# Mixture-of-experts block on one core: maxima first in the prologue, q in long rows, the scale in the selecting matrix, the best sixteen of both tiles at once

## What is computed

```python
att = jnp.einsum('bhqd,bkd->bhqk', q, k) / sqrt(8)          # causal
x = x + softmax(att) @ v @ w_proj                           # x was layer-normed first
q = rmsnorm(layernorm(x)) @ wq.T                            # 2 x 8 heads of 64
sim = jnp.einsum('pbnhd,hkpd->pbnhk', q, keys)              # 2 x 8 x 32 per token
sx, ix = top_k(sim[0], 16); sy, iy = top_k(sim[1], 16)
scores, pk = top_k(sx[..., :, None] + sy[..., None, :], 16) # best 16 of the pairs
h = gelu(xn @ table_down[indices]) * softmax(scores)
out = einsum('bnhk,bnhkd->bnd', h, table_up[indices])
```

## Time and profile before

| | |
|---|---|
| median of 3 runs | 920.95 us (918.83 to 927.84) |
| profiled execution, its own time | 920.11 us |
| its span | 918.3 us |
| busy: PE, DVE, ACT, POOL | 717.5, 758.6, 708.0, 651.5 us |
| first maxima scores start | 31.36 us |
| first exps of attention scores start | 57.32 us |
| first head added on GpSimd in iteration 0 | 131.64 us |
| one iteration of the loop | 49.6 us |

### The profile page before, as it was taken

One profiled execution on the slowest core, in us unless ns is written; L12 is line 12 of the kernel. 1 busy time (PEld: TensorE's weight loads), 2 busy tenths in 40 slices (PEclk: granted clock), 3 DMA queues, 4 the chain that ended last, 5 costly groups with the idle time before them and its releaser, 6 DMA issues.

```text
span 918.3 us, 20833 instructions
## 1 busy us (share of the span) xinstructions
PE 717.5 (78%) x5982; PEld 470.8 (51%) x6014; DVE 758.6 (83%) x2966; ACT 708.0 (77%) x961; POOL 651.5 (71%) x371
## 2 busy tenths in 40 slices
PE   4574578888897979797988889897979797977463
PEld 3433244556474646464655646474646465554323
DVE  3225379989999989898989999998989898979676
ACT  1334388888988989898989889888889898867381
POOL 2012058798797969696979879797969695968662
PEclk9778788999999999999999999999999999888687
DMA  5411312122130403031212112040303121000000
GB/s 158 56 20 29 43 18 51 25 42 38 24 55 10 70 3 67 10 62 18 56 24 50 30 28 52 11 69 9 64 6 62 17 54 24 23 8 19 0 1 11
DMA packets 58160, 32.53 MB, mean 35 GB/s; under 512 B 5904, under 2 KB 57744, under 8 KB 57936
## 3 DMA queue, kind: packets, MB, share of 16 engines
q1 hardware_dynamic: 58128, 32.14, 19.4%
HBM read 19.93 MB, written 5.24 MB: 27 GB/s over the span
## 4 chain that ended last, share of the span: by engine, by line
PE 26%; issue 25%; DVE 24%; ACT 10%; POOL 10%; DMA 1%; SPq 1%; DVEq 1%; POOLq 0%; ACTq 0%
DVE prob L1010 8%; POOL acc L499 6%; PE score L1308 5%; ACT prob L707 4%; DVE late_scores L865 3%; PE misc L1232 2%; PE misc L1331 2%; PE score L1323 2%; ACT late_scores L595 2%; PE score L1271 2%; PE score L1212 2%; DVE halves L859 2%; DVE ranked L909 1%; PE misc L1259 1%; DVE cand L958 1%
## 5 line engine op out<-in xcount | busy, mean ns | idle before, releaser
L499 POOL TENSOR_TENSOR acc<-acc,prob 128x1024 f32<-128x1024 f32 x186 | 442.5, 2379 | 16.6 <-DVE prob L1010 0.5
L1010 DVE SCALAR_TENSOR_TENSOR prob<-score,cut,prob 128x1024 f32<-128x1024 f32 x256 | 317.9, 1279 | 24.6 <-ACT prob L707 23.3
L707 ACT ACTIVATE prob<-score,neg_lse,unit 128x1024 f32<-128x1024 f32 x256 | 301.5, 1202 | 21.9 <-PE score L1308 19.6
L1308 PE MATMUL score<-sel,pieces_t 128*128 128x512 f16 x512 | 164.4, 407 | 62.5 <-DVE prob L1010 59.1
L499 POOL TENSOR_TENSOR acc<-prob 128x1024 f32<-128x1024 f32 x31 | 73.2, 2361 | 103.5 <-DVE prob L1010 103.5
L612 ACT ACTIVATE probs<-score 128x512 f32<-128x512 f32 x192 | 110.4, 596 | 46.5 <-PE score L1214 42.5
L1308 PEld LDWEIGHTS score<-sel,pieces_t 128*128 128x128 f16 x512 | 40.0, 102 | 128.1 <-DVE prob L1010 115.1
L1271 PE MATMUL score<-xn_kept,wdt 128*128 128x128 f32 x480 | 85.0, 278 | 3.9 <-DVE prob L1010 3.5
L1271 PEld LDWEIGHTS score<-xn_kept,wdt 128*128 128x128 f32 x480 | 72.4, 191 | 29.7 <-issue 6.7
L1214 PE MATMUL score<-cb 128*128 128x256 bf16 (+1 forms) x192 | 60.7, 316 | 26.6 <-DMA q_stack<-max_t 17.0
L1182 PE MATMUL score<-k_ahead,q_ahead 128*128 128x256 bf16 (+1 forms) x512 | 70.7, 251 | 10.5 <-DMA q_ahead<-q_scratch 8.3
(11 more groups left out here) (130 smaller groups left out, 1402.3 us busy)
## 6 DMA issues: line engine op xcount, KB each, us to landing
q_ahead<-q_scratch SPq DMA_DIRECT2D x96, 64.0 KB
q_stack<-q_scratch SPq DMA_DIRECT2D x96, 64.0 KB
q_scratch<-qk_piece SPq DMA_DIRECT2D x16, 192.0 KB, 2.4
xin<-x SPq DMA_DIRECT2D x16, 128.0 KB, 4.2
xres<-x SPq DMA_DIRECT2D x16, 128.0 KB, 4.7
x_kept<-x SPq DMA_DIRECT2D x16, 128.0 KB, 2.0
out<-fin SPq DMA_DIRECT2D x16, 128.0 KB, 5.6
xn_kept<-xn_t SPq DMA_DIRECT2D x15, 128.0 KB, 2.0
```

The costliest lines, as they stand in the source:

```text
L499: eng.tensor_tensor(acc[:, j, :], so_far, prob[:, j * FH + h, :], ALU.add).then_inc(acc_added, 1)
L707: eng.activation(prob[:, g, :], score[g % BUFS][:, :], ACT.Exp, bias=neg_lse[:, j, h:h + 1], scale=unit[:, :]).then_inc(prob_made, 1)
L1010: eng.scalar_tensor_tensor(prob[:, g, :], score[g % BUFS][:, :], cut[:, j, h:h + 1], prob[:, g, :], ALU.is_ge, ALU.mult).then_inc(prob_mas ...
L1308: ins = eng.matmul(score[g % BUFS][:, cols], pieces_t[:, j, h, :], sel[:, cols], start=True, stop=True)
```

## The change

Three things, in the words of the code.

The prologue: the row of maxima (`place_max_row`) is issued before the pieces of the next batch are stored; x of batch 2 is loaded before `stack_pieces(0)`; POOL makes the low piece of batch 0 before the norm of batch 1; the first batch's k copies into `k_ahead` are issued by ACT (`first_keys_ahead`); DVE folds the maxima of batch 0 ahead of the remainder of batch 1; the projection of batch 2 stands ahead of batch 0's key scores; `place_tops(0)` stands ahead of the attention exps of iteration 0; `keep_busy` goes from 40 matmuls to 30.

Long rows: the columns of `w_attn` are reordered on the way in so that heads are inside the width, and `q_scratch` is stored piece by piece. Each row of `q_ahead` and `q_stack` is then one run of 8 KB, and three transfers (of 24, 16 and 8 rows) take the place of six.

The scale and the best sixteen: `unit` is rounded to a power of two and multiplied into a bf16 copy of `sel` (`sel_unit`), so L707 loses its scale operand and `cut` is scaled by one small new instruction (`scale_cut`). `shift_best`, `best_exp`, `sum_best`, `log_sum` and `log_sum_exp` each do both tiles at once; three DVE instructions less and one more (`scale_cut`) per iteration. `ln1` goes ahead of `norm_x2`, and the small instructions move to other places.

```diff
-        q_scratch = nc.dram_tensor("q_scratch", (P, 3, T), BF16, kind="Internal").ap()
+        q_scratch = nc.dram_tensor("q_scratch", (3, P, T), BF16, kind="Internal").ap()
...
-                view = q_scratch.rearrange("(h d) s t -> s d h t", d=HD)
-                for c in range(len(Q_PIECE)):
-                    eng.dma_start(q_ahead[c * HD:(c + 1) * HD, :, :], view[Q_PIECE[c]]).then_inc(ahead_in, 16)
+                rows = q_scratch.rearrange("s (d h) t -> (s d) (h t)", d=HD)
+                for c, count in Q_RANGES:
+                    eng.dma_start(q_ahead[c * HD:(c + count) * HD, :, :].rearrange("r h t -> r (h t)"),
+                                  rows[0:count * HD]).then_inc(ahead_in, 16)
...
                 store_pieces(0)
                 look_ahead(0)
+                load_x(2)
                 stack_pieces(0)
                 load_residual(0)
-                load_x(2)
+                place_max_row(0)
                 store_pieces(1)
                 look_ahead(1)
-                place_max_row(0)
                 stack_pieces(1)
+                place_max_row(1)
                 store_pieces(2)
                 look_ahead(2)
-                place_max_row(1)
...
                 make_xhat(0)
+                qk_low_piece(0)
                 make_xhat(1)
-                qk_low_piece(0)
+                make_xhat(2)
                 qk_low_piece(1)
-                make_xhat(2)
...
+            def first_keys_ahead():
+                eng.wait_ge(stack_cleared, 4)
...
+                for c in range(len(K_PIECE)):
+                    eng.dma_start(k_ahead[c * HD:(c + 1) * HD, :],
+                                  qk_piece[D - 2 * HD:D - HD, K_PIECE[c], T:2 * T]).then_inc(ahead_in, 16)
...
-                eng.activation(prob[:, g, :], score[g % BUFS][:, :], ACT.Exp, bias=neg_lse[:, j, h:h + 1],
-                               scale=unit[:, :]).then_inc(prob_made, 1)
+                eng.activation(prob[:, g, :], score[g % BUFS][:, :], ACT.Exp,
+                               bias=neg_lse[:, j, h:h + 1]).then_inc(prob_made, 1)
...
+            def scale_cut(b):
...
+                eng.tensor_scalar(cut[:, :, :], cut[:, :, :], unit[:, :], None, ALU.mult).then_inc(cut_scaled, 1)
...
-                    ins = eng.matmul(score[g % BUFS][:, cols], pieces_t[:, j, h, :], sel[:, cols],
+                    ins = eng.matmul(score[g % BUFS][:, cols], pieces_t[:, j, h, :], sel_unit[:, cols],
                                      start=True, stop=True)
...
-                keep_busy(score[1], 40)
+                keep_busy(score[1], 30)
...
-                xn_transpose(0, y_t_made, 0)
-                key_scores(0, 0, x2_made, 0)
+                eng.wait_ge(y_t_made, every(y_t_made, 0))
+                project_qkv(2, x2_made, 0)
+                xn_transpose(0, v_next_made, 2)
+                eng.wait_ge(qk_high, every(qk_high, 2))
+                key_scores(0, 0, qk_rest_made, 2)
                 key_scores(0, 1, xn_t_made, 0)
-                eng.wait_ge(sim_kept, every(sim_kept, 0))
-                project_qkv(2, v_copied, 1)
-                max_transpose(1, v_next_made, 2)
+                max_transpose(1, sim_kept, 0)
```

191 lines of the change are left out of this document (109 added, 82 removed).

## The result

The change made the kernel faster by half of what was forecast: 898.59 us, median of 4 runs (895.45 to 900.57), against 919.95 us for the kernel before (4 runs beside them); the ratio is 0.9749, 95% interval 0.9706 to 0.9792. The forecast was 878.0 us (868 to 891).

What follows compares the result with a forecast made beforehand. Transfer waits were taken to bound the prologue, a closed chain through GpSimd, ACT, TensorE and DVE the loop. From 920.1 us, 31.7 for the prologue and 10.6 for loop and tail gave 877.8, say 878 (868 to 891).

Steps and rivals of the forecast that it cites:

- rival 1: Loop: it gives nothing, since DVE's or ACT's round is longer or contention eats the saving; 888.4 us, chance 0.15.
- A to D: The prologue's four consecutive stages, from q's landing to iteration 0, forecast to save 31.7 us together.
- Stage A: Prologue up to the first maxima scores: earlier store and fewer q transfers start them 6.7 us earlier, at 24.7.
- stage B: Prologue from there to the first attention scores: they start at 41.0, 15.9 us earlier in all.
- Stage C: Prologue up to batch 1's row of maxima: attention 1 starts at 86.1 instead of 101.42, 15.3 us more.
- whatever leaves DVE's part of it shortens the period: Loop: the closed chain of GpSimd, ACT, TensorE and DVE work sets the 49.59 us period; removing DVE work shortens it.
- the 0.70 us: Loop, behind the second gate: `shifted` (0.20) and the first `neg_lse` (0.50) leave DVE's work before the first mask.
- the 0.13: Loop, between two masks: the second `neg_lse` goes, 0.22 us less 0.09 of overlap.
- the 0.47: Loop: saving per period in us, instead of 0.83, if a fold pays the slow `neg_lse`'s 0.36.
- the 0.7: Loop: saving taken per period in us (0.4 to 0.85), over 12 periods 8.4.
- (4): Pair scores: fp16 pieces with a bf16 matrix run in slow passes; near 1100 us, chance 0.03.
- The exp's 0.09 us: Loop, ACT: L707 without its scale operand takes 0.09 us less, 1.4 us of ACT per iteration.

Runs made afterwards that it cites:

- e1: The kernel before with only the changed prologue and the long rows of q, its loop as before: 892.94 us.
- e7: e3 without the sixteen idle matmuls ahead of the key norms in the prologue: 887.40 us.
- e3: The changed kernel plus sixteen idle TensorE matmuls ahead of the transposes of the next norm's rows: 889.93 us.
- e10: e7 with six idle matmuls for two at both places behind the seventh pair scores: 884.17 us.
- e11: e7 with fifty idle matmuls for thirty ahead of the first maxima scores: 886.12 us.
- e8: e1 plus sixteen idle matmuls ahead of the next norm's rows: steady period 49.55 us, median 2 us lower.
- e6: The changed kernel with the scale back in the exp and the cut unscaled, the best sixteen still merged: 909.15 us.
- e4: The changed kernel with the second norm's statistics again ahead of the next first norm's on VectorE: no change in time.
- e16: The changed kernel, without idle matmuls, with neg_lse of both tiles ahead of the first fold of the maxima: 904.67 us.
- e14: e6 plus sixteen idle matmuls in TensorE's rest: 897.58 us, period 49.84 us in two of three.
- e13: e1 with the scale in the selecting matrix, tiles apart, plus sixteen idle matmuls in TensorE's rest: every period 49.72 us.
- e15: The changed kernel with idle matmuls as in e3, e10 and e11, and none ahead of the key norms: 884.11 us.
- e9: e7 with the cut and its scaling computed ahead of the second gate: 889.06 us, period 49.33 us.

## Why the prediction was wrong, and where it was right

898.59 us lies above the range of 868 to 891. The larger part of the miss is the loop, 8.0 us more where 8.4 less were forecast; the smaller is the prologue, 27.6 us for 31.7.

**Bounds and prologue.** The reading of the prologue was right in kind: every forecast start moved the right way, and e1 shows that none of it is lost later (its periods are 49.57 again; its 892.94 us is what rival 1, no gain in the loop, put at 888.4). It was 4 us too much: the stages gave 5.3, 7.4, 14.2 and 0.7 us for the 6.7, 9.2, 15.3 and 0.5 of A to D. Stage A was off by 1.4 us: the first q was issued at 20.49 and not 20.0, and used 5.6 us later, not after 1.1 of issue and 3.6 of landing. In the prologue the step that failed is in stage B: "the key norms, three DVE steps and one matmul, give about 40.8" left out the sixteen idle matmuls in TensorE's queue. They were free while TensorE stood 5.49 us for the row of maxima; with this wait gone they were its next limit, worth 0.5 us (e7 against e3) to 2. Stage C added another 1.1 us: the second fold took 6.1 us (65.2 to 71.3), beside GpSimd's work on the pieces, for 4.5 in before (77.6 to 82.0), and from its end to the attention scores it was 3.3 us where the stage had 2.8. About 2 us of the 4 go with the clock between 26 and 30 us, which was low in the profiled execution and full in others (the runs e10 and e11).

**The loop.** The step that failed is "whatever leaves DVE's part of it shortens the period". Two things were wrong in it.

First, of the 0.70 us that were to leave the stretch from gate to first mask only 0.30 did: `shifted` with 0.20, and 0.1 of the first fold. The merged neg_lse still lies behind the gate at 503.39 - 502.88 = 0.51 us, where the sum had taken 0.50 for gone. With the 0.13 between the masks 0.43 us left in all, near the 0.47 that the prediction had beside its sum for the case that the slow neg_lse's time is paid by a fold.

Second, and larger: the masks behind that stretch weren't costed at all. Before the change they waited little, and the fourth scores, behind the key scores in TensorE's queue, had 1.4 us to spare when the clock was full (e8). The merged order put GpSimd's norm under VectorE's folds, the rows of the norm came 0.9 us later after the gate, TensorE's rest grew from 1.55 to 2.63 us, its clock fell to 1.2 GHz for the key scores in most iterations, and the fourth mask waited. That took 1.7 us of the 51.0 period. e3 gives it back (49.33). e8 shows that the old loop has the slack to take the slow stretch, which there came in about every second iteration; the new one has it in every iteration and no slack. That merging holds the rows back is shown by e6; through which of its moves (VectorE's order, the later `x` on ACT) is not settled, since neither e4 nor e16 undid it. And with the clock held the loop's edits gain 0.22 us per period, so the 0.7 would not have come even then.

**The rivals.** Rival 1 named the right place, the loop gives nothing, but as equal rounds, and none but (4), for another reason, had a loop that gets longer. That is the missing case: a gain in a ring of several engines can move their phases against each other, and its price was in no row of before except the uneven key scores, 1.98 and 2.90 us, which the prediction didn't ask about. Rival 4 is refuted (414 ns). Its sum doesn't follow from its own price either: 2.2 us for each of 16 scores less 6 is 29 us per iteration and not 15. The exp's 0.09 us was right, and e14 against e3 makes it worth 0.5 us per period beside the merging; e13 against e8 shows that without the merging it is worth nothing.

**The tail** gave 1.7 us of the 2.2. The two waits of 8.5 us in all are gone, as forecast. The first add of iteration 14 comes 1.9 us sooner after that of 13 and that of 15 another 1.0, but that of 13 comes 1.4 us later after that of 12.

## What to carry to other kernels

When a wait goes away, list what stood in its shadow on the engine that waited: idle matmuls that cost nothing under a 5.5 us wait cost 0.5 to 2 us without it. Before taking work out of one engine's part of a ring, look for instructions of the other engines whose duration differs from iteration to iteration (here key scores of 1.98 and 2.90 us): they may be near a limit. Here 1.1 us more of rest went with slow key scores in every iteration instead of every second one. Matmuls that do nothing, put into a rest of TensorE behind which its clock fell, were worth about 1% here (898.59 to 889.93 us) for three lines.

## What was not expected of the hardware

- After 2.63 us without a matmul TensorE's granted clock was 0.50 for the next 5.9 us in the loop (key scores 3.69 us for 1.98). With sixteen idle matmuls in the rest it was 1.00 (e3). In before rests of 1.49 to 1.55 us stood ahead of slow key scores (2.77 to 3.28 us) and rests of 1.38 to 1.50 ahead of fast ones.
- The prologue's clock isn't the same in each execution: from 26 to 30 us it was 0.50 to 0.62 in six kernels and 1.00 in nine, with the same or nearly the same instructions ahead in all but e11 and e15 (both 1.00).
- GpSimd's subtraction and product of 128x256 fp32 take 0.62 us each when they begin ahead of VectorE's folds (e13), and 1.24 and 1.49 when a fold runs already; neg_lse on VectorE takes 0.23 ahead of them (e16) and 0.58 beside them. The Trainium skill (SBUF — State Buffer, "SBUF: two separate sides") says that the two engines have a pair of ports in common, which VectorE uses for instructions with two SBUF inputs against a GpSimd instruction that reads SBUF, and that the one which comes second stands until the other's instruction is done. The trace of after fits within 0.2 us: the first fold runs from 501.75 to 502.97, and a subtraction begun at 502.20 that stood until then would end 0.62 later, at 503.6; it ended at 503.44. In e13 the product comes first and ends at 495.08; the fold that began 0.07 us behind it takes 1.64 us for 1.22.
- Folds that depend on each other don't close up when what lies between them goes: 3.39 us for 3.50 after 0.66 us of small instructions, start to start, were moved out (e9).
